# Rounded-half products for the experts' down projection, and a TensorE loop over the shared-expert groups

## What is computed

```python
logits = xf @ Wg
_, topi = jax.lax.top_k(logits, K)
...
for e in range(E):
    h = jax.nn.silu(xf @ W1[e] + b1[e]) * (xf @ W11[e] + b11[e])
    y = y + (h @ W2[e] + b2[e]) * gates[:, e, None]
z = jax.nn.silu(xf @ Ws1 + bs1) * (xf @ Ws11 + bs11) @ Ws2 + bs2
...
x = x + jnp.tanh(g_ffn[0]) * _L0_ffn_ref(_layernorm(x, axis=-1), ...)
```

## Time and profile before

| what | value |
|---|---|
| device time, median of 3 runs | 657.7 us (657.63 to 659.22) |
| the profiled execution, own time | 662.39 us |
| its span, first to last instruction | 660.0 us |
| mean granted TensorE clock in it | 0.951 |
| PE busy | 563.4 us, 85% |
| DVE / ACT / POOL busy | 53% / 32% / 51% |
| chain that ended last: PE, "another core or an unknown queue", DVE, issue | 69%, 10%, 8%, 5% |

### The profile page before, as it was taken

The page is one execution under the profiler, slowest core; times in us unless marked ns, Lnnn a source line. Parts: engine busy times, 40 slices in busy tenths (PEclk is TensorE's granted clock), DMA queues, the critical chain, the costliest instruction groups (busy, mean ns, idle before and its releaser), DMA issues.

```text
span 660.0 us, 11681 instructions
## 1 busy us (share of the span) xinstructions
PE 563.4 (85%) x3146; PEld 445.7 (68%) x3147; DVE 348.3 (53%) x845; ACT 213.5 (32%) x740; POOL 338.4 (51%) x284
## 2 busy tenths in 40 slices
PE   5789898989979990498999999999999998832997
PEld 4456665656657770386888888888888886622876
DVE  5467787777655710124566655665566652101663
ACT  0687687677771100021222222222222221100110
POOL 4477888898793277130446574544547200772000
PEclk9799999999999995599999999999999999975999
DMA  6661000000205022302356776575562101331003
GB/s 231 266 244 33 18 25 25 24 16 24 81 17 223 25 103 103 120 0 77 116 184 245 273 274 226 183 253 203 205 221 82 46 25 34 106 105 43 0 1 127
DMA packets 32319, 76.05 MB, mean 115 GB/s; under 512 B 4896, under 2 KB 21408, under 8 KB 29344
## 3 DMA queue, kind: packets, MB, share of 16 engines
q1 hardware_dynamic: 12944, 51.52, 21.4%
q10 hardware_dynamic: 16272, 15.74, 7.5%
q0 software_dynamic: 3072, 8.39, 4.0%
HBM read 54.93 MB, written 18.61 MB: 111 GB/s over the span
## 4 chain that ended last, share of the span: by engine, by line
PE 69%; another core or an unknown queue 10%; DVE 8%; issue 5%; POOL 3%; ACT 2%; DMA 1%; DVEq 0%; SPq 0%; ACTq 0%; POOLq 0%
PE mid L646 12%; PE big L627 7%; PE big L629 7%; PE big L628 7%; PE work L402 5%; PE last L567 4%; PE work L567 3%; PE big L551 3%; PE big L549 3%; PE big L550 3%; PE mid L637 3%; PE big L431 3%; PE work L417 2%; PE work L611 2%
## 5 line engine op out<-in xcount | busy, mean ns | idle before, releaser
L709 ACT ACTIVATE arena<-big,nmax 128x128 f32<-128x128 f32 x256 | 90.3, 398 | 4.8 <-DVE nmax L880 4.8
L646 PE MATMUL mid<-dring,arena 128*128 x376 | 88.9, 379 | 0.0
L774 ACT ACTIVATE last<-arena 128x512 f32<-128x512 f32 x47 | 28.3, 602 | 185.5 <-DVE arena L1142 185.5
L627 PE MATMUL big<-u_hi,xsT_hi 128*128 x188 | 82.9, 441 | 1.7 <-issue 1.7
L1142 DVE TENSOR_TENSOR arena<-big,bring 128x512 f32<-128x512 f32 x47 | 32.5, 692 | 89.2 <-PE big L629 89.2
L1035 DVE SCALAR_TENSOR_TENSOR arena<-big,bias,arena 128x512 f32<-128x512 f32 x32 | 23.8, 749 | 99.7 <-ACT arena L759 91.8
L567 PE MATMUL last<-dring,arena 128*128 128x256 f32 x128 | 34.2, 415 | 48.6 <-DVE x_all L1046 48.6
L759 ACT ACTIVATE arena<-big,bias 128x512 f32<-128x512 f32 x32 | 21.9, 687 | 163.6 <-PE big L551 82.5
L629 PE MATMUL big<-u_hi,xsT_lo 128*128 x188 | 74.3, 395 | 0.0
L1267 POOL TENSOR_TENSOR u_lo<-arena,u_hi 128x2048 fp32r<-128x2048 f32 x16 | 73.3, 4583 | 1.3
L1251 POOL TENSOR_TENSOR arena<-arena,rinv 128x1024 f32<-128x1024 f32 x32 | 60.7, 1898 | 25.8 <-DVE rinv L888 25.2
(11 more groups left out here) (133 smaller groups left out, 1118.2 us busy)
## 6 DMA issues: line engine op xcount, KB each, us to landing
arena<-up_w_dram SPq DMA_DIRECT2D x16, 1024.0 KB, 7.6
bring<-expert_bias_dram SPq DMA_DIRECT2D x16, 640.0 KB, 5.3
dring<-down_w_dram SPq DMA_DIRECT2D x18, 512.0 KB, 3.4
sorted_y<-arena ACTq DMA_DIRECT2D x47, 128.0 KB, 1.8
arena<-sorted_x ACTq DMA_DIRECT2D x43, 128.0 KB
sorted_x<-dring SPq DMA_DIRECT2D x3, 1536.0 KB, 8.5
dring<-up_w_dram SPq DMA_DIRECT2D x2, 1024.0 KB, 4.9
xf_all<-xfs SPq DMA_DIRECT2D x16, 128.0 KB, 2.0
```

Source lines behind the costliest of these rows:

```text
L627: mm(big[:, p, w, :], x_hi, u_hi[:, slot, o:o + HID], start=(k == 0), stop=False)
L646: i = mm(mid[:, 1, 0:D], gT[:, p, c, :], dring[:, slot, c * D:(c + 1) * D], start=(c == 0), stop=(c == HC - 1))
L709: i = nc.scalar.activation(probs[:, u % 2, h, :], big[:, u % 2, h // 4, (h % 4) * CTX:(h % 4 + 1) * CTX], ACT.Exp, bias=nmax[:, u % 2, h:h ...
```

## The change

**Experts' down.** Each of the 4 f32 products becomes three fp32r products of the same 256 columns: gT_hi with w_hi, gT_hi with w_lo, gT_lo with w_hi. ACT writes gT_hi and posts gT_hi_ready. A new DVE step, hidden_lo(n), subtracts gT_hi from the PSUM tile, writes gT_lo and posts gT_ready. GpSimd splits the down weights too (split_down, two slots), with waits on the load and on down_ps of the expert two earlier. PE's down waits for d_split, and SP's load of down weights waits for the split two experts earlier. The first two experts' down weights are split ahead of the scatters.

**Shared groups.** shared_groups is one loop body for groups 2, 3 and for 5, 6, 7: up(s,0), down(s-1), up(s,1 to 3). gsh has one buffer from group 1 on, so shared_hidden(s) waits for all tiles of down(s-1). DVE's order follows: add_shared(s-1) comes ahead of shared_hidden(s). z_taken starts at 2 by a tiny memset instead of a special case for the first two tiles. Several buffers share storage, and shared down weights always sit in slot 0 of dring.

```diff
+            def shared_groups(first, h):
+                with pe.Fori(first, SGROUPS * (h + 1)) as s:
+                    g = pe.snap(s % SGROUPS)
+                    shared_up(s, g, h, 0)
+                    shared_down(s - 1, h)
+                    for c in range(1, HC):
+                        shared_up(s, g, h, c)
...
-            shared_ups(2)
-            shared_down(1)
-            shared_ups(3)
-            shared_down(2)
+            shared_groups(2, 0)
...
             def down(b, p):
-                slot = pe.snap(item_of(b) % WSLOTS)
+                item = item_of(b)
+                slot = pe.snap(item % DSLOTS)
+                pe.wait_ge(d_split, item)
                 pe.wait_ge(gT_ready, b + 1)
...
-                    i = mm(mid[:, 1, 0:D], gT[:, p, c, :], dring[:, slot, c * D:(c + 1) * D], start=(c == 0), stop=(c == HC - 1))
+                    w_hi, w_lo = d_hi[:, slot, c * D:(c + 1) * D], d_lo[:, slot, c * D:(c + 1) * D]
+                    mm(mid[:, 1, 0:D], gT_hi[:, p, c, :], w_hi, start=(c == 0), stop=False)
+                    mm(mid[:, 1, 0:D], gT_hi[:, p, c, :], w_lo, start=False, stop=False)
+                    i = mm(mid[:, 1, 0:D], gT_lo[:, p, c, :], w_hi, start=False, stop=(c == HC - 1))
...
-            for s in range(5, 8):
-                shared_ups(s)
-                shared_down(s - 1)
-            shared_down(7)
+            shared_groups(5, 1)
+            shared_down(7, 1)
...
                     if s >= 2:
-                        dve.wait_ge(z_ps, GROUP * (s - 1))
+                        dve.wait_ge(z_ps, GROUP * s)
...
+            def hidden_lo(b, p):
+                dve.wait_ge(gT_hi_ready, b + 1)
+                if not (isinstance(b, int) and b < 2):
+                    dve.wait_ge(down_ps, b - 1)
+                v.tensor_tensor(gT_lo[:, p, :, :].rearrange("p c n -> p (c n)"), mid[:, 0, :],
+                                gT_hi[:, p, :, :].rearrange("p c n -> p (c n)"), ALU.subtract).then_inc(gT_ready, 1)
...
                     hidden(n + 1, 1 - p)
+                hidden_lo(n, p)
                 add_out_bias(n - 1, 1 - p)
...
+            def split_down(i, slot):
+                ring = 1 if slot else 2
+                g.tensor_copy(d_hi[:, slot, :], dring[:, ring, :]).then_inc(d_hi_done, 1)
+                pool.wait_ge(d_hi_done, i)
+                g.tensor_tensor(d_lo[:, slot, :], dring[:, ring, :], d_hi[:, slot, :], ALU.subtract).then_inc(d_split, 1)
...
                 split(PIECES + UNITS + i - 2, raw[:, slot, :], slot, 0, 1)
+                if isinstance(i, int):
+                    return
+                pool.wait_ge(w_odd if slot else w_even, 16 * i + (16 if slot else 32))
+                pool.wait_ge(down_ps, end)
+                g.tensor_tensor(pool_mark[:, :], mhalf[:, :], mhalf[:, :], ALU.mult)
+                split_down(i, slot)
```

More of the change, by code:

```diff
@@ L67 @@
 GROUP = 4
+SGROUPS = TILES // GROUP
+ZBANKS = 2
+SHARED = 0
+DSLOTS = 2
 PIECES = UNITS * (PAIRS - 4)
@@ L203, in flamingo_layer @@
         gT_ready = sem("gT_ready")
+        gT_hi_ready = sem("gT_hi_ready")
+        d_hi_done = sem("d_hi_done")
+        d_split = sem("d_split")
         kT_ready = sem("kT_ready")
@@ L552, in shared_up, with shared_down @@
                 i.then_inc(sh_ps, 1)
-            def shared_ups(s):
-                for c in range(HC):
-                    shared_up(s, c)
-            def shared_down(s, tiles=range(GROUP)):
-                slot = (ITEMS - 1) % WSLOTS if s >= TILES // GROUP else 0
+            def shared_down(s, h, tiles=range(GROUP)):
+                first = isinstance(s, int) and s == 0
+                gshT = gsh_first if first else gsh_next
                 for t in tiles:
-                    n = GROUP * s + t
-                    if n >= 2:
-                        pe.wait_ge(z_taken, n - 1)
+                    pe.wait_ge(z_taken, GROUP * s + t + 1)
                     for c in range(HC):
@@ L663, in _ @@
             transpose_rows(0, 0)
-            shared_down(3, range(1))
+            shared_down(3, 0, range(1))
             transpose_rows(1, 1)
@@ L667, in _ @@
             pe.wait_ge(xsT_ready, 2)
-            shared_down(3, range(1, GROUP))
-            pe.wait_ge(z_taken, 4 * GROUP)
+            shared_down(3, 0, range(1, GROUP))
+            pe.wait_ge(z_taken, ZBANKS + 4 * GROUP)
             transpose_rows(2, 2)
@@ L980, in pair @@
                         choose(j - 1)
+            v.memset(zfree[:, :], 0.0).then_inc(z_taken, ZBANKS)
             v.memset(mhalf[:, :], -0.5).then_inc(half_ready, 1)
@@ L1176, in _ @@
             hidden(1, 1)
+            hidden_lo(0, 0)
             for n in range(1, 5):
@@ L1197, in _ @@
             shared_hidden(4, range(HC))
+            add_shared(4)
             shared_hidden(5, range(HC))
-            add_shared(4)
+            add_shared(5)
             for c in range(HC):
@@ L1203, in _ @@
                 combine(2 * c + 1)
-            add_shared(5)
+            add_shared(6)
             for c in range(HC):
@@ L1208, in _ @@
                 combine(GATHERS + 2 * c + 1)
-            add_shared(6)
             add_shared(7)
```

100 lines of the change are left out of this document (54 added, 46 removed).

## The result

The changed kernel takes 662.0 us (661.69 to 662.91, 5 runs), the one before 657.7 (656.88 to 659.22, 5 runs): ratio 1.0066, 95% interval 1.0053 to 1.008. It is slower by 4.3 us, where 3.3 were forecast. One execution of a later run was slow (a_two, 674.67 us at a granted clock of 0.752, the other three 593 to 597) and is left out of every figure.

The account below looks back on a forecast made before the run. PE alone was taken to bound the blocks before, sequencer and DVE after. Terms 1.8 - 1.2 + 1.4 + 0.5 + 1.5 - 0.6 = +3.4 on 657.7 gave 661.1, rounded to 661.0 us; range 646 to 670.

Parts of the forecast that it names:

- the likeliest case: Whole kernel: sequencer and DVE bound the blocks at 5.03 to 5.2 us a slot, 656 to 666 us; chance 0.50.
- Slot time in the blocks: Blocks: 5.10 us a slot instead of 5.13, given as -1.2 us over 45 slots.
- PE's own sum: Blocks: PE's work per slot falls by 0.28 to 0.39 us from 5.13, to 4.75 to 4.84.
- Case D: Experts' down: narrow fp32r products cost nearly as much as wide ones, +26 to +45 us, 684 to 703; chance 0.06.
- case B: Blocks: PE's sum decides instead of the lap, 12.6 to 17.5 us gained there, 643 to 648; chance 0.20.
- the lap: Blocks: chain from an up through DVE's steps and PE's sequencer to the up after next, 10.07 us for two slots.
- Both first splits lie in a gap of GpSimd: nothing: Ahead of the scatters: splitting the first two experts' down weights in GpSimd's idle time costs 0.
- Groups, first half: Shared groups around the scatters: two chunks more and two tiles fewer left at the release, +1.8 us (0 to +4).
- Groups, second half: Shared groups around the gathers: same work left at the release, plus open waits at the end, +1.5 us.
- GpSimd: Blocks: split_down takes 3.65 us per expert, 10.35 in all against 10.25 for a two-block expert, +0.5 us.
- case C: Two-block runs: GpSimd becomes the bound, 0.2 to 0.8 us for each of ten experts, 663 to 669; chance 0.12.
- Tail and fill: Two last experts' downs shorter, -0.6 us; filling and leaving the longer lap once, +1.4 us.

Follow-up runs that it names:

- a_two: Changed kernel without the second of down's three products per chunk (gT_hi with w_lo); 595.22 us, ratio 0.9868 to the kernel before.
- the run with both cures: Changed kernel with the first two down splits after the scatters and down's expert loaded ahead of the gT_ready wait; 651.2 us, ratio 0.9896 to before.
- Run f: Changed kernel without the product of gT_hi with w_lo in each chunk of down; 595.22 us, ratio 0.9868 to the kernel before.
- run e: Changed kernel with down's expert loaded and its addresses worked out ahead of PE's wait for gT_ready; 599.06 us, ratio 0.9915 to the kernel before.
- run d: Changed kernel with hidden_lo(n) ahead of hidden(n+1) in DVE's order; ratio 1.0053 to the kernel before.
- b: Changed kernel with the first two experts' down weights split after the scatters instead of ahead of them; 658.85 us, ratio 0.9999 to the kernel before.
- the kernel before, again: The kernel before, unchanged, run for a second profile; 658.0 us against 658.5, ratio 0.9993.
- a_again: The changed kernel run again as it is; 662.18 us, ratio 1.0057 to the kernel before.
- c: Changed kernel with DVE's small table copies written as a maximum of a value with itself; ratio 1.0075 to the kernel before.
- a_f32: Changed kernel with the experts' down as before (4 f32 products, no hidden_lo, no down split), groups' loop kept; 602.55 us, ratio 0.9997 to before.
- a_late: Changed kernel with the first two experts' down splits moved behind the scatters, nothing else; 658.85 us, ratio 0.9999 to the kernel before.

## Why the prediction was right, and where it was not

**The total**: +3.3 was forecast and +4.3 measured. The range, the sign and the likeliest case hold.

**Slot time in the blocks: right.** T = 5.10 was taken, and 229.61 / 45 = 5.10 came out; the stretch is +0.7, as forecast. PE has idle time in front of the ups (402.99 above, 0.41), in every second slot, not in each one. The sum itself has a slip: 45 x (5.10 - 5.13) is -1.35, not -1.2.

**PE's own sum: right, at its upper end.** In the run with both cures two of the loop's four slots take 4.84 (4.75 to 4.84 forecast), the others 4.93 and 4.98; in the changed kernel none is under 4.93. The 12 narrow products come every 0.12 us and the down's stretch is 1.5 us, 0.2 of it the first one:

```profile
417.86 0.36 PE L656 MATMUL mid<-d_hi,gT_hi 128*128 x1
418.06 0.28 PE L657 MATMUL mid<-d_lo,gT_hi 128*128 x1
418.18 0.28 PE L658 MATMUL mid<-d_hi,gT_lo 128*128 x1
...
419.25 0.28 PE L658 MATMUL mid<-d_hi,gT_lo 128*128 x1
419.37 0.40 PE L634 MATMUL big<-u_hi,xsT_hi 128*128 x1
```

Those 1.51 us from the first of them to the next up are above the 1.34 to 1.45 forecast, and hardly below the 1.54 of before: most of what the slot gained shows at the up's own first product, behind which the second starts 0.24 us later, where it was 0.42 behind an f32 product. The estimate by the figure of the Trainium skill ("TensorE: Matmul & The Clock Gate", section "Wait — 56ns, not 53.3ns?"), 0.109 a product and 1.31 for twelve, isn't reached either. Case D (narrow products as dear as wide ones) is out, and case B would have meant 4.84 a slot.

**Why the lap binds: right.** The sum 3.31 + 2.68 + 0.68 + 3.4 = 10.07 fits the pairs of slots measured (4.93 + 5.16 = 10.09), and part by part: DVE's 3.31 + 2.68 + 0.68 = 6.67 against 6.66, the sequencer's 3.4 against 3.44. Only the loop's branch was put too high, at 0.5: the laps with it are 10.35, 0.26 longer. Run f shortened the sequencer's part and the lap by the same 0.46, run e took it below PE's own time and gave 7.1 us. The expectations of e read run d as a sign that DVE's part doesn't count; g_ready at 420.34 shows that d had left that part as long as it was. The prediction's sentence that a product's own wait frees the sequencer isn't borne out at this place: the transposes carry the wait for g_ready themselves, and the sequencer's next record still comes 0.06 us after it is posted.

**"Both first splits lie in a gap of GpSimd: nothing": wrong.** The step that failed looked at GpSimd's own idle time and not at what another engine does in it. It is +4.05 in the profiles, the largest term of all, and taking it out (b) gave back all of the slowdown.

**Groups, first half, +1.8: right in the changed kernel, but no fixed cost.** When PE resumes after the first standstill, six chunks (each the 12 products of a shared_up) and five tiles of down are left in all four profiles with early splits on these chips, and four and seven in the kernel before, again: two chunks more and two tiles fewer, as counted. From there to up 0 it is 29.5 instead of 26.9 us (+2.6, +2.4 forecast), and PE resumes 46.5 instead of 47.3 after the first transfer (-0.8, -0.6 forecast). With both cures the late posts fall otherwise: one more chunk starts at 253.48, five are left, and the stretch takes 72.87 and 73.54, where the order of before takes 73.79. With late splits alone it is 74.66. The forecast's "from 0, if the late posts fall otherwise" covers this. So the early splits cost something here too, 1.3 us or more. Why they change the posts stays open, and no run has them with the order of before on a chip with standstills.

**Groups, second half, +1.5: not borne out.** What is left was counted right again (ten chunks and twelve tiles instead of eight and fourteen), and from the release to the end it is 54.5 instead of 52.5, +2.0. But PE resumes 44.3 us after the first gather, where it was 47.1: 2.7 sooner, 0.6 forecast, so the stretch is shorter by 0.8. That moment moves by itself, 44.3 to 47.1 in seven profiles with the loop. These gave 98.8 to 101.1 for the whole stretch, the order of before 99.6, 100.4 and 100.8 in three, which is no difference. In the whole time the order is worth 0 within about 1.3 us (ratio 0.9897 against 0.9896).

**GpSimd: small and mis-sized.** Its step for down weights takes 3.60 (from mark 335.32 to mark 338.92) where 3.65 was worked out. The idle time of 3.1 us that the row of a_again puts down to it doesn't measure it, since the profile gives such a name to the last post that it knows of: at 402.99 it names GpSimd, where the sequencer was late. The starts show it better. In four slots of the first third PE's sequencer passes its wait for the split up weights (L625) 0.04 us after GpSimd's subtract ends, and these take 6.03, 5.32, 5.86 and 5.29, in sum 1.4 us more than the lap, against +0.5 forecast. With both cures the same four are still GpSimd's (5.77, 5.37, 5.90, 5.28), 2.7 us in sum, though the row of that run doesn't name it. The first of them:

```profile
348.28 4.62 POOL L1289 TENSOR_TENSOR u_lo<-arena,u_hi 128x2048 fp32r<-128x2048 f32 x1
...
L625 PEldq FUSED_REGOPS  x1: 96/96/96, 352.9 to 352.9; - x1
```

So case C, GpSimd as the bound, came true in four experts of the ten that it named, for 1.4 us instead of 2 to 8. It is what is left to gain in the blocks.

**Tail and fill: right.** -0.6 forecast for the last downs, -1.0 measured; the fill, +1.4 forecast: from up 1 to up 3 9.88 against 8.47. The 45 slots hold it, so that the others are on average 0.02 shorter than before.

So the errors, measured less forecast, were +4.05 for the early splits, -2.3 for the end after the gathers and -0.4 for the last downs, and what they left is 1.4 us in the profiles, 1.0 in the medians. That the total came out within 1 us is luck, and shows nothing about its terms.

## What to carry to other kernels

Before work is put into an engine's gap, look at what the other engines do in that gap, not only whether this one is idle: small steps of VectorE that touch only SBUF wait there for the end of GpSimd's long ones. Where an engine's sequencer stands at a wait, put its table loads and address arithmetic ahead of it; here 0.86 us of steps moved by two lines turned a change that was 0.66% slower, with the other cure, into one that is 1.0% faster. When an edit swaps two steps, check first whether the consumer needs both: then it takes nothing out. And take a second profile of the kernel before, if its first one lies off the median by as much as the effect that is looked for.

## What was not expected of the hardware

**Held VectorE steps**: 0.17 to 0.20 us became 0.90 to 2.28 beside GpSimd's steps of 1.3 to 2.5 us (b, c).

**The standstills depend on the chip.** On one chip the kernel before takes 604 us, on the others 658. All of the difference lies in the two stretches of indirect transfers: from the first transfer to up 0, 47.98 (a_f32) against 74.21, and from the gathers' first to the end 72.82 against 99.58, which is 26.2 + 26.8 = 53 us. Busy time over these two stretches, first on that chip (run e), then with standstills (the changed kernel again):

```profile
229.30:277.20 47.90, 45.71 (x209) 38.52 (x207) 14.62 (x26) 7.70 (x11) 35.30 (x34) 1.00 0.33 114
526.10:597.60 71.50, 68.21 (x296) 56.83 (x296) 33.11 (x64) 9.66 (x14) 30.98 (x32) 0.98 0.30 88
```

```profile
228.90:305.10 76.20, 51.30 (x209) 41.48 (x207) 15.26 (x28) 7.69 (x11) 34.99 (x34) 0.84 0.26 94
561.20:660.30 99.10, 69.40 (x296) 56.94 (x296) 33.06 (x64) 9.63 (x14) 30.74 (x32) 0.88 0.21 64
```

PE does the same work (209 and 296 products) in 45.7 of 47.9 us there, and in 51.3 of 76.2 here. GpSimd issues the same transfers in the same time on both. What is late are the posts of TensorE's products: in the changed kernel the last product of a chunk starts at 255.48, and ACT's silu on it at 274.42. PE resumes 45.7 to 47.3 us after the first scatter in nine profiles of ten on these chips (in a_late one chunk comes through at 34), so the end of the standstill goes with the transfers. What delays the posts on some chips and not on the other isn't shown by any row; 50 us of this kernel hang on it.
